# A fused attention, norm, routing and experts kernel: block loops written out, rows loaded ahead of weights, padding and two transposes moved

## The reference, cut to what matters

```python
qkv = x @ qkv_w + qkv_b                       # heads of 3 * 16 columns
q, k = rot(q), rot(k)                         # rotary, angle by head
attn = softmax(einsum('bhqd,bhkd->bhqk', q, k) / 4)
x1 = layernorm(x + einsum('bhqk,bhkd->bhqd', attn, v) @ out_w + out_b)
n = layernorm(x1) * g1 + be1
x2 = x1 + n + (n @ mix_w + mix_b)
n = layernorm(x2) * g2 + be2
probs = softmax(n @ router_w)                 # top 2 of 8 experts
out = sum over the two experts e: probs[e] * (silu(n @ w1[e] + b1[e]) @ w2[e] + b2[e])
y = layernorm(x1 + x2 + out)
```

## Time and profile before

| | us |
|---|---|
| median of 3 runs | 1795.01 (1794.37 to 1795.82) |
| the profiled execution | 1798.72 |
| its span | 1796.9 |
| TensorE matmul busy | 1654.3 (92%) |
| ScalarE busy | 1251.4 (70%) |
| VectorE busy | 413.3 (23%) |
| GpSimd busy | 490.3 (27%) |

### The profile page before, as it was taken

One profiled execution on the slowest core, in us unless ns is written; L12 is line 12 of the kernel. 1 busy time (PEld: TensorE's weight loads), 2 busy tenths in 40 slices (PEclk: granted clock), 3 DMA queues, 4 the chain that ended last, 5 costly groups with the idle time before them and its releaser, 6 DMA issues. The chain is left out here.

```text
span 1796.9 us, 49277 instructions
## 1 busy us (share of the span) xinstructions
PE 1654.3 (92%) x18140; PEld 953.3 (53%) x18141; DVE 413.3 (23%) x1380; ACT 1251.4 (70%) x1863; POOL 490.3 (27%) x512
## 2 busy tenths in 40 slices
PE   5986999999999999999999999999998979999990
PEld 3642333333333333334334334458988969999990
DVE  3441001521512412413313324315310000000004
ACT  2436899998999989999999999973433433444432
POOL 4750000111121211210220221223444433444441
PEclk9997999999999999999999999999999999999995
DMA  3568300101110345310110110555566565556645
GB/s 117 186 154 116 65 23 20 35 18 37 34 31 25 66 73 86 86 45 11 34 44 11 34 44 11 191 166 145 154 176 177 174 178 167 177 177 175 177 125 193
DMA packets 104749, 177.77 MB, mean 99 GB/s; under 512 B 11994, under 2 KB 78618, under 8 KB 104378
## 3 DMA queue, kind: packets, MB, share of 16 engines
q1 hardware_dynamic: 91250, 157.20, 29.8%
q0 software_dynamic: 13296, 17.77, 6.2%
HBM read 134.59 MB, written 40.18 MB: 97 GB/s over the span
## 5 line engine op out<-in xcount | busy, mean ns | idle before, releaser
L1091 ACT ACTIVATE place<-at_s 128x1024 f32<-128x1024 f32 x1024 | 968.3, 1065 | 81.9 <-PE at_s L1172 74.1
L1172 PE MATMUL at_s<-place 99*32 99x512 bf16 x8192 | 576.5, 383 | 25.4 <-ACT place L1091 16.8
L1184 PE MATMUL at_po<-place,at_v 128*32 128x512 f32 x4096 | 540.7, 599 | 8.8 <-issue 8.0
L1172 PEld LDWEIGHTS at_s<-place 99*32 99x32 bf16 x8192 | 205.3, 96 | 477.0 <-issue 282.1
L1329 PE MATMUL at_s<-place 128*128 x1136 | 261.4, 384 | 7.0 <-issue 5.5
L1316 PEld LDWEIGHTS at_s<-place 128*128 128x128 f32 x2272 | 264.3, 192 | 4.1 <-issue 0.8
L1316 PE MATMUL at_s<-place 128*128 128x128 f32 x2272 | 265.5, 275 | 0.0
L1108 ACT ACTIVATE place<-at_s,b_turned 128x128 f32<-128x128 f32 x568 | 161.8, 368 | 141.6 <-PE at_s L1316 141.6
L1329 PEld LDWEIGHTS at_s<-place 128*128 128x128 f32 x1136 | 212.1, 192 | 38.1 <-issue 11.4
L1184 PEld LDWEIGHTS at_po<-place,at_v 128*32 128x32 f32 x4096 | 126.8, 112 | 114.2 <-issue 9.2
L1124 ACT ACTIVATE place<-at_s,at_v 128x256 f32<-128x256 f32 x71 | 33.6, 473 | 181.3 <-PE at_s L1329 181.3
(11 more groups left out here) (203 smaller groups left out, 978.6 us busy)
## 6 DMA issues: line engine op xcount, KB each, us to landing
place<-in_w SPq DMA_DIRECT2D x79, 1024.0 KB, 5.5
place<-k_parts SPq DMA_DIRECT2D x48, 256.0 KB, 10.0
place<-q_parts SPq DMA_DIRECT2D x192, 64.0 KB
at_v<-rows_in SPq DMA_DIRECT2D x71, 129.0 KB, 4.6
x_in<-in_x SPq DMA_DIRECT2D x9, 512.0 KB, 4.6
q_parts<-qk_lower SPq DMA_DIRECT2D x16, 256.0 KB, 2.3
k_parts<-qk_lower SPq DMA_DIRECT2D x16, 256.0 KB, 2.5
rt_x_in<-in_x SPq DMA_DIRECT2D x8, 512.0 KB, 3.9
```

Source lines behind the costliest of these rows:

```text
L1091: nc.scalar.activation(probs[:, slot(n), :], p_s[n % BUFFERS][:, :], ACT.Exp).then_inc(exp_done, 1)
L1172: last = nc.tensor.matmul(p_s[n % BUFFERS][j:j + 32, s * 512:(s + 1) * 512], k_rows[0:ROWS_M, quad(q).start + h, kt * P + j:kt * P + j + 3 ...
L1184: last = nc.tensor.matmul(p_o[32 * h:32 * h + 32, :], v_one[q % 2][:, h, kt, :], probs[:, slot(q * NG + g), s * 512:(s + 1) * 512], start= ...
```

## The change

Five edits:

- The loops over groups 1 to 6 on TensorE, VectorE and GpSimd, and over groups 1 to 7 on ScalarE, are Python loops, so that every group has its own code.
- In `load_turn` a tile's rows are loaded ahead of its weights.
- SyncE's loop over turns is cut in two: turns 1 to 3 (tiles 6 to 23) first, then the last group's sum and the padding, then turns 4 and 5 (tiles 24 to 35). The waits for the padding, for `sent` and for the second plan stay ahead of tile 36.
- On TensorE the first norm's two transposes are at steps 52 and 58 instead of 50 and 56.
- The second norm's first transposes are at step 82 instead of 80. `TAIL_AT` names the new steps at the same points.

```diff
--- before.py
+++ after.py
@@ -775,8 +775,8 @@
         LAST = GROUPS - 1
         EARLY_TURNS, TURNS = EARLY // XR, -(-TILES // XR)
         TAIL_TURNS = 3
-        TAIL_AT = {0: (12,), 1: (18,), 2: (24, 26), 3: (30, 32), 9: (50,), 10: (56,), 11: (60, 62), 12: (64, 68),
-                   17: (80,), 18: (86,), 19: (90, 92), 26: (118,)}
+        TAIL_AT = {0: (12,), 1: (18,), 2: (24, 26), 3: (30, 32), 9: (52,), 10: (58,), 11: (60, 62), 12: (64, 68),
+                   17: (82,), 18: (86,), 19: (90, 92), 26: (118,)}
         ROUTER_AFTER, SEND_AFTER = 10, 15
 
         def slot(n):
@@ -924,10 +924,10 @@
 
                 def load_turn(turn, tiles):
                     for r in range(tiles):
+                        load_rows(turn * XR + r, r)
                         load_w1(turn * XR + r, r % W1_RING)
-                        load_rows(turn * XR + r, r)
-
-                with sp.Fori(1, EARLY_TURNS) as turn:
+
+                with sp.Fori(1, TAIL_TURNS + 1) as turn:
                     load_turn(turn, XR)
                 keep_sum(LAST)
 
@@ -937,6 +937,8 @@
                     sp.dma_start(dram["rows_in"][bass.ds(end, P), 0:D], zero_rows[:, :]).then_inc(padded, 16)
                     sp.dma_start(dram["rows_in"][bass.ds(end, P), D:ROW], pad_home[:, e, :].bitcast(F32)
                                  ).then_inc(padded, 16)
+                with sp.Fori(TAIL_TURNS + 1, EARLY_TURNS) as turn:
+                    load_turn(turn, XR)
                 sp.wait_ge(padded, 32 * E)
                 sp.wait_ge(sent, GROUPS + 1)
                 sp.wait_ge(planned, 2)
@@ -1014,7 +1016,7 @@
                 pool.sem_inc(sent, 1)
                 pool.sem_inc(x_biased, 1)
                 pool.sem_inc(kept_stored, 16)
-                with pool.Fori(1, GROUPS - 1) as i:
+                for i in range(1, GROUPS - 1):
                     for q in range(UNITS):
 
                         copy_v(i * UNITS + q + 1, ((i + (q + 1) // UNITS) // QC, (q + 1) % UNITS))
@@ -1134,7 +1136,7 @@
                     scale_y(i, r)
 
                 exponentials(0, False)
-                with act.Fori(1, GROUPS) as i:
+                for i in range(1, GROUPS):
                     exponentials(i, True)
                 act.sem_inc(h_ready, 4)
                 act.sem_inc(y_scaled, 2)
@@ -1242,15 +1244,15 @@
                     elif at in OUT_AT:
                         half, first = OUT_AT[at]
                         return product(out_w, (2 * half, 2 * half + 1), D, job, (first, first + 1))
-                    elif at == 50:
+                    elif at == 52:
                         pe.wait_ge(norm1_ready, i + 1)
                         turn(norm1, 0, job)
-                    elif at == 56:
+                    elif at == 58:
                         turn(norm1, 1, job)
                     elif at in MIX_AT:
                         half, first = MIX_AT[at]
                         return product(mix_w, (2 * half, 2 * half + 1), D, job, (first, first + 1))
-                    elif at == 80:
+                    elif at == 82:
                         pe.wait_ge(norm2_ready, i + 1)
                         turn(sent_rows[:, 0, :, 0:D], 0, job)
                     elif at == 86:
@@ -1293,7 +1295,7 @@
                 attend(0, False, False, 0)
                 pe.wait_ge(loaded_w, 16 * 9)
                 pe.wait_ge(constants_ready, 8)
-                with pe.Fori(1, GROUPS - 1) as i:
+                for i in range(1, GROUPS - 1):
                     attend(i, True, False, first_job(i))
 
                 def turn_x(turn, r, i):
@@ -1529,7 +1531,7 @@
                     copy_out(0, q)
                     divide(0, q, job)
                 dve.wait_ge(loaded_w, 16 * 9)
-                with dve.Fori(1, LAST) as i:
+                for i in range(1, LAST):
                     job = Job(first_job(i))
                     steps = Chain(dve, step, (i - 1) * STEPS)
                     copy_out(i - 1, UNITS - 1)
```

## The result

| | before | after |
|---|---|---|
| median of 4 runs, us | 1795.41 (1794.37 to 1800.34) | 1745.26 (1741.69 to 1745.75) |
| profiled execution, its span | 1798.72, 1796.9 | 1745.3, 1743.5 |

The ratio is 0.9714, 95% interval 0.9695 to 0.9733. The forecast was 1751.5, with 1740 to 1768 as its range.

What follows compares the result with a forecast made beforehand. TensorE's matmul issue was taken as the bound, with ScalarE's exponentials close behind. Savings of 18.7 + 10.0 + 8.8 + 6.0 = 43.5 us gave 1755.2 profiled, 1751.5 as median; 8 in 10 within 1740 to 1768.

Steps and rivals of the forecast that it cites:

- Part 1: Attention groups: writing out the block loops removes the engines' jumps back; 18.7 us saved, bounds 12 and 21.3.
- Part 2: Norm transposes at steps 52, 58 and 82: TensorE no longer waits for VectorE; 10.0 us saved, bounds 5 and 11.2.
- Part 3: Expert tiles 17 to 35: rows sent ahead of weights land before TensorE asks; 8.8 us saved, bounds 4 and 11.
- Part 4: Padding after tile 23 instead of 35: old cost 15.0, new 9.0; 6.0 us saved, bounds 4 and 10.
- The jump is not what costs: Rival at group ends: they are slow for another reason, such as the scatters; loops give nothing, 1770 us, chance 0.07.
- Code runs dry: Rival in attention: fetching written-out code stops TensorE, as perhaps in group 3; slower, 1814 us at five a group, chance 0.03.
- The later transposes give nothing: Rival in attention: ScalarE sets the pace or VectorE's chain is late at step 60; 1761.5 us, chance 0.08.
- the experts give nothing: Rival in the expert tiles: rows stay late from contention and the padding stall only moves; 1766 us, chance 0.09.
- Padding hidden: Rival at tile 24: its rows land in time, so moving the padding gives 15 us; 1742.5 us, chance 0.06.

Runs made afterwards that it cites:

- the expectation of 10 us for 25: Changed kernel with only TensorE's loop over groups 1 to 6 put back: 1755 us expected, 1770.62 us measured, 25 us more than the changed kernel.
- the kernels with one loop: Changed kernel with one engine's loop put back: TensorE's over groups 1 to 6, 1770.62 us; ScalarE's over groups 1 to 7, 1754.17 us.
- the single changes: Kernel before with only the norms' transposes later, 1783.58 us; with only a tile's rows loaded ahead of its weights, 1779.47 us.
- the spread padding: Changed kernel with one pair of padding writes behind the loads of each of tiles 24 to 31: 1735.72 us, ratio 0.9659.

## Why the prediction was right, point by point

**Part 1, the loops.** 18.7 us forecast at the ends and inside, with 2.6 more left in group 3. At the ends the sum before is 109.3 (five of them 19.14, 17.62, 19.20, 17.28, 19.50, and 16.56), after 92.0: 17.3. The end without jumps, put together as 15.41, measured 15.33. The sum was right because it came from lengths, not from waits. The price of a single jump in the text was not: TensorE's 2.2 us is what shows beside ScalarE's own late start, and alone it is about 3.2 us of stop, and 4.4 us of time in the mean with what the clock adds. That one jump covers the other was not seen; a kernel with only one loop written out would have been forecast badly, as the expectation of 10 us for 25 shows. The stop in group 3, which was left standing, went (group 3: 115.75 to 111.65, the others 1.8): 2.3 us more than forecast. It was a late fetch of code, as the prediction suspected. That it would go was not foreseen, so these 2.3 us are luck. VectorE's and GpSimd's jumps cost nothing, as said.

**Part 2, the transposes.** 10.0 forecast beside what part 1 counted. Group 7, which had no jump of TensorE before either, went from 112.85 to 111.28: 1.57 against 1.43. The chain to step 60 fits. That a us less wait is a us less time held; alone the change gave 13 (8 to 18) against 11.2.

**Part 3, the rows.** 8.8 forecast for tiles 17 to 35; measured 9.35 there outside the stop (139.76 to 43.47 + 14.49 + 72.45, the stop's pair taken as even). Outside of them the tiles 3 to 17 gave 3.9 and 37 to 70 gave 2.1, which had stood only in the upper bound. This is the term that was too small: 15.4 us instead of 8.8. The reason was the choice of the stretch, not the mechanism: by the loads alone the same three stretches gave 15.2. (In tiles 3 to 17 only 1.1 to 3.9 us are the order's, as the old order took 114.7 to 117.0 there.) The rows were to leave some 4 us earlier. Those of tile 23 now go at 1318.31, 11.8 us ahead of their transposes at 1330.15, where the prediction had 6.9: 4.9 us.

**Part 4, the padding.** New cost 9.0 forecast, 9.45 measured. Its terms: rows 24 go 17.7 us after the weights of 23 (1323.24 to 1340.94) against 16.9; they land in 2.3 us, not 4.1, with no weights ahead of them; lateness 5.7 against 6.8; the clock takes 3.8 rather than 2.2. Two errors, of 1.1 and 1.6 us, went opposite ways, so that the sum came so close is luck; other traces of the same stop have 7.5 to 9.8. What fell is the attribution: the 15.0 - 9.45 = 5.6 us are not the new place's. The order of the loads alone took 4.5 of them, and the place added 1.1 in this trace; the place alone took 5.1. Each shortens the same lateness.

**Sum.** From the two spans: attention 32.4 against 28.7, experts from tile 3 to the last 3.9, 14.9 and 2.1, together 21.0, against 14.8, the first stage 0.8 less and the last 0.8 more. That is 53.4 us between the profiled executions, 9.9 more than the 43.5 forecast: 3.7 in attention (the stop, the transposes and the lower ends) and 6.2 in the experts, nearly all from tiles not counted. The medians differ by 50.2, since the execution profiled before was 3.3 us slower than its median. So the time is 6.2 us under the forecast, and inside its range.

**Rivals.** "The jump is not what costs" fell by the kernels with one loop. "Code runs dry" read the stop in group 3 rightly, but needed 21 more of them; there is one fewer. "The later transposes give nothing" and "the experts give nothing" fell by the single changes. "Padding hidden" did not happen, but the spread padding shows that it can.

## What to carry to other kernels

Take a moved or removed step's worth from the length of a stretch that has it against one that hasn't, and not from the wait shown, since two engines' waits can lie over each other. A loop's jump back matters on the engine that sets the pace: here one of TensorE's cost 2.5 us, or 4 to 6 with the clock. Those of engines that wait there anyway cost nothing, and neither did TensorE's between expert tiles (tiles 25 to 35 ran at 7.245 us each with two jumps among them). A group has some 3560 instructions of TensorE and six tiles some 600; whether the length of the body is what decides was not tested. When an engine stops with no releaser, look at the instruction queue's packets beside it. Eight pairs of writes (128 KB and 1 KB) in a row on the queue that feeds the bound engine stopped it at both places tried; spread one pair to a load, they cost nothing.

## What the runs showed that was not expected

- TensorE stops of 0.7 to 2.1 us inside group 3 (in one kernel also in group 4) behind a flood of key loads, in all eight profiled kernels with a loop of TensorE (group 3 is 1.2 to 4.2 us longer inside than its neighbours there) and in none of the five without (0.1 to 0.4). Each follows a fetch of code that came late. Why as late a fetch stops nothing in the other five is open.
- Behind a stop of 3 us TensorE's granted clock fell to 1.2 GHz at four of five ends and stayed up at the fifth, for the same code: 1.8 to 3.1 us of difference an end. In the kernel before it fell at the ends of groups 1, 3 and 5 (19.14, 19.20, 19.50 us) and stayed up at those of 2 and 4 (17.62, 17.28).
- 129 KB of rows landed in 2.1 us in the median (page of the kernel after) where they had taken 4.6. The order alone gave 2.7; the ten kernels with the rows ahead have 2.1 to 2.8 and the three with the weights ahead 4.6 or 4.7. So the megabyte just ahead of them in the same queue is what had made them slow.
